# The product x2 W2 moved to the head of a neighbour search, with the loads behind the search reordered

## The chip, the cores and the metric

The kernel runs on one core of a Trainium2 chip. The metric is the device time of one execution in microseconds (us). Before the change the median of three runs is 1454.12 us (1453.49 to 1454.47).

## What is computed

Four graph layers in a row on x, 4096 nodes by 128 features, with a dense 4096 x 4096 matrix A. Each has the form x <- layernorm(x + layer(x)). The third and the fourth are the ones that matter here:

```
# layer 2: x2 goes in, x3 comes out
z   = leaky_relu(lap(A, x2) @ W1 + b1)                 # lap(A, x) = d * (A @ (d * x)), d = rowsum(A)^-1/2
S   = exp(-dist(z, z) / 2), kept for the 4 nearest rows of each row, else 0
out = lap(S + A, x2) @ W2 + b2                         # d from rowsum(S + A)
x3  = layernorm(x2 + out)
# layer 3
x4  = layernorm(x3 + relu(concat(x3, A @ x3) @ W.T + b))
```

## The kernel before

**Products.** The kernel makes six products with A, numbered 0 to 5 in the code (`p`); product five is `p = 4` (A with the scaled x2) and product six is `p = 5` (A with x3). Every f32 operand is split in a high and a low f16 half, so a tile of 128 rows of A costs three matmuls (L1144 to L1146) for each chunk of 512 output columns. There are 32 row tiles (`kt`) and 8 chunks. The first 7 row tiles of A stay in SBUF (`kept`); the other 25 lie in HBM (`at_scratch`) and are loaded either as units of 5 tiles (1280 KB, `load_late`, L417) into a ring of 5 slots, or as single tiles (256 KB, L428) into 8 tile slots.

**Search.** Between product four and five stands the search for the 4 nearest rows: 32 rows of tiles, `i` = 0 to 31. For each row TensorE makes 8 banks of closeness values (`first_banks`, `second_banks`, L1297 to L1299 and L1304), ScalarE (ACT) copies the banks from PSUM to SBUF (`copy_near`, L682), and VectorE (DVE) takes the 8 largest of each line and their places (`search`, L1028 and L1029). From row 8 on TensorE does beside it the first four chunks of product five (`wide_products`, row tile `i - 8`), whose operand becomes known four row tiles at a time: a group `g` of four rows goes through POOL (`distances`, `degree_sums`, `scales`, `low_y`), ACT (`weights`, `degrees`, `high_y`) and DVE (`inverse`), and the scaled x2 is written in two f16 halves, `yop`.

**x2 W2.** The sparse part of the product needs rows of (d * x2) W2 in HBM (`y_scratch`). In the kernel before it is made group by group during the search: POOL loads x2 (`load_x2`, L501), TensorE transposes it (`pe_turn`, L1093), ACT copies the transpose (L712), TensorE multiplies by W2 (`pe_project_x2`, L1120), ACT scales by d (`scale_yw`, L729) and POOL stores it (L548). The last group's part of this stands behind the search.

**Behind the search.** POOL loads x2 once more as residual (four loads, L558), and then issues 128 gathers of rows of `y_scratch` (L569), 16 for each chunk. DVE mixes them chunk by chunk: `mix_tile` (L837, L839), `close_mix` (layernorm and the split in halves, L798 and L799, which make product six's operand), and `residual` (L831), which reads the projected product five from PSUM. TensorE makes the rest of product five, chunks 4 to 7 (`chunk_columns`), and at places written out by hand (`PROJECT4_AT`) the projection of a finished chunk by W2 (`pe_project`, L1113). `pe_project` of chunk c waits until DVE's `residual` has read chunk c - 1 (`nat_read`); `RESIDUAL_AT` puts `residual` of chunk 3 behind the first mixed tile of chunk 1:

```python
RESIDUAL_AT = {(0, 2): [0], (0, 3): [1], (0, 4): [2], (1, 1): [3], **{(c, 3): [c + 3] for c in range(1, 5)}}
```

SP's queue carries the single tiles and all units in one order; the first three units stand between the tiles of the last rows (`LATE_AT`), the others wait until the first four chunks are done and the last group of y is stored.

Of the kernel before, what the change touches and what calls it, by code (L numbers as in the profile page):

```python
# [21 lines left out]
F32 = mybir.dt.float32  # L22
# [7 lines left out]
P = 128  # L30
# [13 lines left out]
LATE_ORDER = [4, 3, 2, 0, 1]  # L44
# [6 lines left out]
WIDE_AT = {i: i - 8 for i in range(8, 32)}  # L51
# [6 lines left out]
PROJECT4_AT = {(4, 9): 0, (4, 15): 1, (4, 21): 2, (4, 28): 3, (5, 12): 4, (6, 12): 5, (7, 12): 6}  # L58
# [3 lines left out]
WIDE_REST = [24, 25, 26, 27, 28, 29, 30, 31]  # L62
LATE_AT = {29: 0, 30: 1, 31: 2}
# [4 lines left out]
Y_SCALE = {-1: 256.0, 0: 16.0, 1: 128.0, 2: 512.0, 3: 512.0, 4: 128.0}  # L68
# [3 lines left out]
def gnn_kernel(nc, x, adj, d_list, w0, filt, bias0, alpha, w1, b1, wz, bz, w2, b2, w3, b3, out):  # L72
# [14 lines left out]
    y_dram = nc.dram_tensor("y_scratch", [N, D], F32).ap()  # L87
    part_dram = nc.dram_tensor("part_scratch", [NCH, P, CHUNK], F32).ap()

    with ExitStack() as ctx:  # L90
# [33 lines left out]
        x2_in = [chunk_buffer(s) for s in range(2)]  # L124
        yw = [chunk_buffer(2 + s) for s in range(2)]
        assert (REGION_TILES + 4) * tile_elems <= near_end - 4 * N

# [82 lines left out]
        util_nat = pt[3][:, :].rearrange("p (t f) -> p t f", t=TPC)  # L210
# [36 lines left out]
        dinv_ready, yhi_ready, yw_full, yw_ready = sem("dinv_ready"), sem("yhi_ready"), sem("yw_full"), sem("yw_ready")  # L247
        x2_loaded = [sem(f"x2_loaded{b}") for b in range(2)]
# [96 lines left out]

        block = ctx.enter_context(nc.Block())
# [3 lines left out]
        def _(sp):  # L350
# [61 lines left out]
            def load_late(k):  # L412
                p, c, u = LATE[k]
                slot = LATE_SLOTS[k]
                if slot in LATE_SLOTS[:k]:
                    sp.wait_ge(*late_released(max(b for b in range(k) if LATE_SLOTS[b] == slot)))
                sp.dma_start(ring[slot].rearrange("p k h n -> p (k h n)"), at_dram[c, u, :, :]  # L417
                             ).then_inc(late_loaded_unit[slot], 16)
# [27 lines left out]
        def _(pool):  # L446
# [53 lines left out]
            def load_x2(g):  # L500
                pool.dma_start(x2_in[g % 2], rows(x_dram[2], g)).then_inc(x2_loaded[g % 2], 16)  # L501

            pool.wait_ge(acc_full, 4 * NCH)
            load_x2(0)
            load_x2(1)
# [25 lines left out]
            def scales(g_tiles, g):  # L531
                pool.wait_ge(dinv_ready, g + 1)
                nc.gpsimd.tensor_tensor(S[:, g_tiles, :], S[:, g_tiles, :], dinv2[:, g_tiles].unsqueeze(2)
                                        .to_broadcast([P, TPC, TOP]), ALU.mult).then_inc(S_scaled, 1)

            def low_y(g_tiles, g):
                pool.wait_ge(yhi_ready, g + 1)
                pool.wait_ge(xT_full, nth(XT, 4, g))
                x2 = x2_in[g % 2]
                step(nc.gpsimd.tensor_tensor(x2, x2, dinv2y[:, g_tiles].unsqueeze(2).to_broadcast([P, TPC, D]), ALU.mult))  # L540
                nc.gpsimd.tensor_tensor(yop[1][:, 1, g_tiles, :], x2, yop[1][:, 0, g_tiles, :], ALU.subtract
                                        ).then_inc(yop_ready, 1)

            for g in range(NCH):
                for stage_of in (distances, degree_sums, scales, low_y):
                    stage_of(slice(g * TPC, (g + 1) * TPC), g)
                pool.wait_ge(yw_ready, g + 1)
                pool.dma_start(rows(y_dram, g), yw[g % 2]).then_inc(y_stored[g % 2], 16)  # L548
                if g + 2 < NCH:
                    pool.wait_ge(yop_ready, nth(YOP, "y", g))  # L550
                    pool.wait_ge(xT_full, nth(XT, 4, g))
                    load_x2(g + 2)


            pool.wait_ge(near_full, KT * NCH)
            x2_rows = x_dram[2].rearrange("(c t p) f -> p t c f", p=P, t=TPC)
            for t in range(TPC):
                pool.dma_start(res_rows(t // 2, 0, NCH)[:, :, t % 2, :], x2_rows[:, t, :, :]).then_inc(res_loaded, 16)  # L558
# [52 lines left out]
        def _(act):  # L611
# [96 lines left out]
            def turned_x2(g):  # L708
                act.wait_ge(xT_full, nth(XT, 4, g))
                if g > 0:  # L710
                    act.wait_ge(yw_full, g)
                nc.scalar.activation(xT[:, :], late_turn[:, :], ACT.Copy).then_inc(xT_ready, 1)  # L712

            def high_y(g):
                act.wait_ge(dinv_ready, g + 1)
                act.wait_ge(x2_loaded[g % 2], 16 * (g // 2 + 1))
                for t in range(TPC):
                    kt = g * TPC + t
                    last = nc.scalar.activation(yop[1][:, 0, kt, :], x2_in[g % 2][:, t, :], ACT.Copy,
                                                scale=dinv2y[:, kt:kt + 1])  # L720
                last.then_inc(yhi_ready, 1)

            def scale_yw(g):
# [770 lines left out]
```

## Time and profile before

| | before |
|---|---|
| median of 3 runs | 1454.12 us |
| time of the profiled execution | 1455.45 us |
| its span, first to last instruction | 1453.9 us |
| mean granted clock of TensorE | 0.990 |
| PE busy | 1392.0 us (96%) |
| DVE busy | 836.8 us (58%) |
| ACT busy | 450.9 us (31%) |
| POOL busy | 249.0 us (17%) |
| HBM | 277 GB/s over the span |

The span is one profiled execution; 1.5 us of its time lie around it. PE is TensorE's matmuls. A matmul's own time is longer than its distance to the next one, since they are pipelined, so the stages are read from starts and from idle time. Granted clock 1.00 is 2.4 GHz and 0.50 is 1.2 GHz.

### The profile page before, as it was taken

The page shows a single profiled execution, that of the slowest core. Times are in us where ns is not written, and L with a number is a line of the kernel's source. Part 1 is how long each engine was busy: PE and PEld are TensorE (multiplying, and loading weights), DVE is VectorE, ACT ScalarE, POOL GpSimd, SP SyncE. Part 2 cuts the span into 40 slices and gives each one's busy share as a digit, 9 for nine tenths or more (in the row PEclk, how much of TensorE's full clock was granted, in tenths as well). Part 3 has the DMA queues.
Part 4 walks back from the last instruction along what each step waited for, and adds up shares of the span by engine and source line. Part 5 has one row for each costly group of instructions (what it writes and reads, how often), then busy time and mean ns, then how long its engine had stood idle before and what let it go on. Part 6 is the DMA issues. An engine that isn't in the chain of part 4 may idle for free.

```text
span 1453.9 us, 20144 instructions
## 1 busy us (share of the span) xinstructions
PE 1392.0 (96%) x7300; PEld 738.1 (51%) x7300; DVE 836.8 (58%) x1311; ACT 450.9 (31%) x979; POOL 249.0 (17%) x358
## 2 busy tenths in 40 slices
PE   6999999999999999999999987999999889999997
PEld 4666676666544444444445432444444344444454
DVE  6877766666223523333222379999999356555044
ACT  4666665655200000000000045666666200000011
POOL 2111110110101100000000000111111277774000
PEclk9999999999999999999999999999999989999999
DMA  9999998897999979988878420004444799999961
GB/s 302 394 375 391 352 326 322 316 308 256 356 385 364 350 282 398 396 324 323 307 278 326 190 73 1 15 30 131 131 131 123 249 377 397 374 396 392 353 247 57
DMA packets 112818, 403.32 MB, mean 277 GB/s; under 512 B 10368, under 2 KB 28384, under 8 KB 91232
## 3 DMA queue, kind: packets, MB, share of 16 engines
q1 hardware_dynamic: 72672, 314.33, 58.2%
q0 software_dynamic: 20576, 77.07, 14.1%
q10 hardware_dynamic: 19488, 10.80, 2.4%
q8 instruction: 54, 0.88, 0.2%
q14 instruction: 28, 0.23, 0.0%
HBM read 337.67 MB, written 64.49 MB: 277 GB/s over the span
## 4 chain that ended last, share of the span: by engine, by line
PE 77%; DMA 10%; DVE 9%; ACT 1%; issue 1%; ACTq 0%; SPq 0%; DVEq 0%; POOL 0%; POOLq 0%
PE acc L1144 10%; PE acc L1146 9%; PE acc L1145 9%; PE pt L1208 5%; PE pt L1146 5%; PE pt L1145 5%; PE pt L1144 5%; DMA region<-in_adj 4%; PE pt L1297 3%; PE pt L1299 3%; PE pt L1298 3%; DVE hT L1028 3%; DMA region<-at_scratch 3%; PE acc L1189 2%; PE acc L1191 2%; PE acc L1193 2%
## 5 line engine op out<-in xcount | busy, mean ns | idle before, releaser
L1208 PE MATMUL pt<-ident,region 128*128 128x128 f32 x1024 | 243.8, 278 | 21.4 <-DMA region<-in_adj 12.9
L1144 PE MATMUL acc<-region,yop 128*128 128x512 f16 x581 | 221.3, 381 | 10.9 <-DMA region<-at_scratch 10.9
L1146 PE MATMUL acc<-region,yop 128*128 128x512 f16 x581 | 221.2, 381 | 0.0
L1145 PE MATMUL acc<-region,yop 128*128 128x512 f16 x581 | 221.2, 381 | 0.0
L974 DVE SCALAR_TENSOR_TENSOR region<-pt,region 128x512 f16<-128x512 f32 x200 | 135.5, 687 | 77.0 <-ACT region L636 76.7
L1208 PEld LDWEIGHTS pt<-ident,region 128*128 128x128 f32 x1024 | 146.2, 143 | 64.2 <-issue 14.7
L682 ACT ACTIVATE region<-pt 128x512 f32<-128x512 f32 x256 | 132.8, 603 | 109.5 <-PE pt L1304 95.8
L636 ACT ACTIVATE region<-pt 128x512 f16<-128x512 f32 x200 | 117.5, 595 | 108.3 <-PE pt L1208 89.4
L1028 DVE MAX8 hT<-region 128x8 f32<-128x4096 f32 x32 | 141.2, 4411 | 2.4 <-ACT region L682 2.4
L603 ACT ACTIVATE std<-mv,eps_ln 128x4 f32<-128x4 f32 x32 | 9.5, 297 | 343.0 <-DVE mv L808 343.0
L1297 PE MATMUL pt<-yop 128*128 128x512 f16 x256 | 97.3, 380 | 15.5 <-ACT region L682 15.5
L1144 PEld LDWEIGHTS acc<-region,yop 128*128 128x128 f16 x581 | 56.9, 98 | 80.6 <-issue 11.7
L1298 PE MATMUL pt<-yop 128*128 128x512 f16 x256 | 97.0, 379 | 0.0
L1299 PE MATMUL pt<-yop 128*128 128x512 f16 x256 | 97.0, 379 | 0.0
L469 POOL DMA_DIRECT2D at_scratch<-region x80 | 42.7, 534 | 314.2 <-DVE region L974 304.5
L1144 PE MATMUL pt<-region,yop 128*128 128x512 f16 x250 | 94.8, 379 | 0.0
L1145 PE MATMUL pt<-region,yop 128*128 128x512 f16 x250 | 94.8, 379 | 0.0
L1146 PE MATMUL pt<-region,yop 128*128 128x512 f16 x250 | 94.8, 379 | 0.0
L1146 PEld LDWEIGHTS acc<-region,yop 128*128 128x128 f16 x581 | 57.0, 98 | 69.2 <-issue 1.1
L1145 PEld LDWEIGHTS acc<-region,yop 128*128 128x128 f16 x581 | 56.9, 98 | 62.5 <-issue 0.3
L986 DVE TENSOR_REDUCE rs_part<-region 128x1 f32<-128x512 f32 x128 | 86.5, 676 | 0.0
L1193 PE MATMUL acc<-region,yop 128*128 128x512 f16 x200 | 75.8, 379 | 0.0
(236 smaller groups left out, 2239.6 us busy)
## 6 DMA issues: line engine op xcount, KB each, us to landing
region<-at_scratch SPq DMA_DIRECT2D x166, 1280.0 KB, 8.1
region<-in_adj SPq DMA_DIRECT2D x64, 1024.0 KB, 9.3
at_scratch<-region POOLq DMA_DIRECT2D x40, 768.0 KB, 7.1
at_scratch<-region POOLq DMA_DIRECT2D x40, 512.0 KB, 7.6
region<-at_scratch SPq DMA_DIRECT2D x76, 256.0 KB, 2.8
x_scratch<-xout ACTq DMA_DIRECT2D x16, 256.0 KB, 13.7
gath_all<-x_scratch POOLq DMA_DIRECT2D x12, 256.0 KB, 6.6
xin<-at_scratch SPq DMA_DIRECT2D x12, 256.0 KB, 2.7
```

The source lines that it names most:

```text
L636: nc.scalar.activation(dst, pt[kt % 4][:, :], ACT.Copy, scale=A_SCALE).then_inc(high_done, 1)
L682: nc.scalar.activation(near[i % 2][:, j * CHUNK:(j + 1) * CHUNK], near_bank(i, j)[:, :], ACT.Copy).then_inc(near_copied, 1)
L974: nc.vector.scalar_tensor_tensor(lo, pt[kt % 4][:, :], A_SCALE, hi, ALU.mult, ALU.subtract).then_inc(low_done, 1)
L1028: step(nc.vector.max(top8[:, i, :], near[i % 2]))
L1144: nc.tensor.matmul(into, y[:, 0, kt, :], high, start=(kt == first_tile), stop=False)
L1145: nc.tensor.matmul(into, y[:, 0, kt, :], low, start=False, stop=False)
L1146: return nc.tensor.matmul(into, y[:, 1, kt, :], high, start=False, stop=(kt == last_tile))
L1193: last = nc.tensor.matmul(acc[par][:, :], yl, hi, start=False, stop=(kt == KT - 1))
L1208: ins = nc.tensor.transpose(pt[kt % 4][:, t * P:(t + 1) * P], nat[u % 4][:, t, (kt % TPC) * P:(kt % TPC + 1) * P], ident[:, :])
L1297: nc.tensor.matmul(into, zh, zT[:, 0, cols], start=True, stop=False)
L1298: nc.tensor.matmul(into, zh, zT[:, 1, cols], start=False, stop=False)
L1299: nc.tensor.matmul(into, zl, zT[:, 0, cols], start=False, stop=False)
```

## The change

x2 W2 is made without the scaling by d in search rows 1 to 4, stored in a new HBM tensor (`xw_scratch`) and loaded again group by group. The scaled rows (d times it) now serve both as the rows that are gathered and as product five's operand, so product five comes out already multiplied by W2 and `pe_project` only transposes it. The wide columns lag the search by 7 rows and not 8. The four residual loads go from POOL's queue to SP's; units 0 to 3 go from SP's queue to ACT's; two units of chunk 4 are used between the wide rows; `inverse` and `high_y` come one row earlier. The core of the diff:

```diff
-LATE_ORDER = [4, 3, 2, 0, 1]
+LATE_ORDER = [4, 3, 2, 1, 0]
...
-WIDE_AT = {i: i - 8 for i in range(8, 32)}
+WIDE_LAG = 7
+WIDE_AT = {i: i - WIDE_LAG for i in range(WIDE_LAG, 32)}
...
-PROJECT4_AT = {(4, 9): 0, (4, 15): 1, (4, 21): 2, (4, 28): 3, (5, 12): 4, (6, 12): 5, (7, 12): 6}
+PROJECT4_AT = {(4, 17): 0, (4, 21): 1, (4, 25): 2, (4, 29): 3, (5, 12): 4, (6, 12): 5, (7, 12): 6}
...
-LATE_AT = {29: 0, 30: 1, 31: 2}
+ACT_LATE = 4
+RES_AT = 26
@@ SP
+            sp.wait_ge(z_ready, NCH)
+            for g in range(NCH + 2):
+                if g > 0 and g < NCH:
+                    sp.wait_ge(xT_full, nth(XT, 4, g - 1))
+                if g < NCH:
+                    sp.dma_start(t_nat[:, :, :], rows(x_dram[2], g)).then_inc(x2_loaded, 16)
+                if g >= 2:
+                    sp.wait_ge(xw_ready, g - 1)
+                    sp.dma_start(rows(xw_dram, g - 2), xw_out[g % 2]).then_inc(xw_stored[g % 2], 16)
...
             for kt in range(KEPT, KT):
+                if kt == RES_AT:
+                    sp.wait_ge(near_full, KT * NCH)
+                    for t in range(TPC):
+                        sp.dma_start(res_rows(t // 2, 0, NCH)[:, :, t % 2, :], x2_rows[:, t, :, :]).then_inc(res_loaded, 16)
...
-                if kt in LATE_AT:
-                    sp.wait_ge(near_used, KT - 1 if LATE_AT[kt] == 0 else KT)
-                    load_late(LATE_AT[kt])
...
             sp.wait_ge(acc_full, nth(ALL, 4, WIDE - 1))
-            sp.wait_ge(yop_ready, nth(YOP, "y", NCH - 1))
-            sp.wait_ge(xT_full, nth(XT, 4, NCH - 1))
-            for b in range(2):
-                sp.wait_ge(y_stored[b], 16 * NCH // 2)
-            for k in range(len(LATE_AT), len(LATE)):
-                load_late(k)
+            for k in range(ACT_LATE, len(LATE)):
+                load_late(sp, k)
@@ POOL
             for g in range(NCH):
-                for stage_of in (distances, degree_sums, scales, low_y):
+                for stage_of in (distances, degree_sums, scaled_y, low_y, scales):
                     stage_of(slice(g * TPC, (g + 1) * TPC), g)
-                pool.wait_ge(yw_ready, g + 1)
                 pool.dma_start(rows(y_dram, g), yw[g % 2]).then_inc(y_stored[g % 2], 16)
...
-            pool.wait_ge(near_full, KT * NCH)
-            for t in range(TPC):
-                pool.dma_start(res_rows(t // 2, 0, NCH)[:, :, t % 2, :], x2_rows[:, t, :, :]).then_inc(res_loaded, 16)
@@ ACT
+            def copy_xw(g):
+                act.wait_ge(xw_full, g + 1)
+                if g >= 2:
+                    act.wait_ge(xw_stored[g % 2], 16 * (g // 2))
+                nc.scalar.activation(xw_out[g % 2].rearrange("p t f -> p (t f)"), acc[1][:, :], ACT.Copy, scale=Y_SCALE[3]
+                                     ).then_inc(xw_ready, 1)
...
+            def projection_step(k):
+                if 0 < k <= NCH:
+                    copy_xw(k - 1)
+                if k < NCH:
+                    turned_x2(k)
...
+            projection_step(0)
+            for i in range(1, KT + TPC + 1):
+                if i == KT:
+                    act.wait_ge(near_used, KT - 1)
+                    load_late(act, 0)
+                if i == KT + 1:
+                    act.wait_ge(near_used, KT)
+                    load_late(act, 1)
+                    load_late(act, 2)
...
+                projection_step(2 * i - 1)
                 if i < KT:
                     copy_near(i, COPY_ORDER[NEAR_BANKS:])
+                projection_step(2 * i)
...
+            act.wait_ge(yop_ready, nth(YOP, "y", NCH - 1))
+            for b in range(2):
+                act.wait_ge(y_stored[b], 16 * NCH // 2)
+            load_late(act, ACT_LATE - 1)
@@ TensorE
-                if p == 1:
+                if p in (1, 4):
                     last = nc.tensor.transpose(into[:, t, :], h, ident[:, :])
...
             for i in range(1, KT):
                 first_banks(i)
+                projection_step(2 * i - 1)
+                if i == WIDE_LAG:
+                    pe.wait_ge(xw_ready, NCH)
                 if i in WIDE_AT and i < KT - 1:
                     wide_products(WIDE_AT[i], range(WIDE // 2))
                 second_banks(i)
+                projection_step(2 * i)
...
+            kept_narrow(NARROW_KEPT[0])
+            wide_products(25)
+            kept_narrow(NARROW_KEPT[1])
+            wide_products(26)
+            wide_products(27)
+            chunk_columns(4, WIDE, range(KEPT, KEPT + 2 * UNIT))
+            for kt in range(28, KT):
                 wide_products(kt)
```

On TensorE `projection_step(k)` multiplies group k - 1 by W2 (`pe_project_x2`) and transposes group k (`pe_turn`).

## Rows read from the trace of the kernel before

**Rows 1.** Windows by stage: busy us (count) per engine, clock, DMA share, GB/s.

```profile
851.50:914.00 62.50, 47.45 (x248) 18.47 (x247) 62.18 (x24) 33.76 (x68) 3.94 (x10) 1.00 0.02 7
914.00:1120.00 206.00, 205.60 (x1080) 89.70 (x1078) 204.87 (x82) 129.48 (x264) 31.10 (x70) 1.00 0.32 98
1120.00:1146.00 26.00, 25.04 (x127) 12.45 (x128) 17.69 (x8) 12.57 (x30) 7.11 (x14) 1.00 0.43 136
1146.00:1175.00 29.00, 17.92 (x54) 5.44 (x53) 2.53 (x3) 0.53 (x1) 14.46 (x16) 0.73 1.01 355
1175.00:1284.00 109.00, 109.00 (x534) 53.85 (x533) 69.91 (x161) 5.74 (x13) 84.01 (x83) 0.99 0.99 385
1284.00:1384.00 100.00, 100.00 (x469) 45.90 (x467) 31.31 (x72) 2.08 (x5) 37.07 (x39) 1.00 0.97 377
```

**Rows 2.** Windows again: two stretches at a lowered clock.

```profile
1156.00:1169.00 13.00, 9.10 (x21) 2.50 (x21) 0.00 (x0) 0.00 (x0) 6.70 (x7) 0.50 1.03 380
1173.00:1177.00 4.00, 4.00 (x11) 1.42 (x12) 3.93 (x4) 0.60 (x1) 3.63 (x2) 0.58 0.96 369
```

**Rows 3.** Timeline of DVE, search: start, us, line, operation, tiles, [idle before].

```profile
851.55 4.43 DVE L1028 MAX8 hT<-region 128x8 f32<-128x4096 f32 x1 [2.42 <-ACT region L682]
...
1132.99 4.42 DVE L1029 FIND_INDEX8 wT<-hT,region 128x8 uint32<-128x4096 f32 x1
1141.81 0.18 DVE L1034 RECIPROCAL inv_deg<-dinv 128x4 f32<-128x4 f32 x1 [4.40 <-ACT dinv L706]
```

**Rows 4.** Timeline of PE, row one of the search.

```profile
854.69 0.39 PE L1297 MATMUL pt<-yop 128*128 128x512 f16 x1 [0.68 <-ACT region L682]
...
858.95 0.39 PE L1297 MATMUL pt<-yop 128*128 128x512 f16 x1 [1.17 <-ACT region L682]
```

**Rows 5.** Timeline of PE, behind the search: one of six waits.

```profile
1156.14 0.61 PE L1144 MATMUL acc<-region,yop 128*128 128x512 f16 x1 [2.91 <-DMA region<-at_scratch]
```

**Rows 6.** Timeline of POOL, behind the search.

```profile
1143.58 1.04 POOL L540 TENSOR_TENSOR region<-region,scale 128x512 f32<-128x512 f32 x1 [1.09 <-ACT yop L719]
...
1145.80 0.82 POOL L548 DMA_DIRECT2D y_scratch<-region  x1
1146.62 2.67 POOL L558 DMA_DIRECT2D yop<-x_scratch  x3
1160.46 0.90 POOL L558 DMA_DIRECT2D yop<-x_scratch  x1 [11.18 <-issue]
1161.67 1.06 POOL L569 DMA_INDIRECT gath_all<-y_scratch,wz_sb  x1 [0.31 <-issue]
...
1183.58 0.94 POOL L569 DMA_INDIRECT gath_all<-y_scratch,wz_sb  x1 [0.30 <-issue]
```

**Rows 7.** Source view of L548, stores of y.

```profile
DMA to landing us min/median/max: 2.8/2.8/5.7
```

**Rows 8.** Timeline of DVE, first mixed chunk.

```profile
1189.87 0.69 DVE L837 TENSOR_TENSOR gath_all<-gath_all,bias 128x512 f32<-128x512 f32 x1 [2.43 <-DMA gath_all<-y_scratch,wz_sb]
...
1197.00 0.74 DVE L799 SCALAR_TENSOR_TENSOR yop<-xout,yop 128x512 f16<-128x512 f32 x1
...
1199.34 1.12 DVE L831 SCALAR_TENSOR_TENSOR yop<-pt,inv_deg,yop 128x128 f32<-128x128 f32 x4
```

**Rows 9.** Timeline of PE, projection of chunk four in product five.

```profile
1200.86 1.05 PE L1113 MATMUL pt<-w_sb,hT 128*128 128x128 f32 x8
```

**Rows 10.** Chain of waits, a projection: start, us, what.

```profile
1201.02 0.89 PE pt L1113 x8
```

**Rows 11.** Chain of waits, four transposes in place of one.

```profile
402.02 0.44 PE pnat L1107 x4
```

**Rows 12.** DMA issues from 840 to 1200: queue, count, KB each, us to landing.

```profile
region<-at_scratch SPq DMA_DIRECT2D x10, 1280.0 KB, 9.9
...
region<-x_scratch POOLq DMA_DIRECT2D x8, 256.0 KB, 3.5
...
yop<-x_scratch POOLq DMA_DIRECT2D x4, 512.0 KB, 10.3
```

More of the change, by code:

```diff
@@ L122, in chunk_buffer @@
             return region[:, at:at + tile_elems].bitcast(F32).rearrange("p (t f) -> p t f", t=TPC)
-        x2_in = [chunk_buffer(s) for s in range(2)]
+        xw_in = [chunk_buffer(s) for s in range(2)]
         yw = [chunk_buffer(2 + s) for s in range(2)]
         assert (REGION_TILES + 4) * tile_elems <= near_end - 4 * N
+        xw_out = [tiles[REGION_TILES - 2 + s].rearrange("p h n -> p (h n)").bitcast(F32)
+                  .rearrange("p (t f) -> p t f", t=TPC) for s in range(2)]
         yop = [sb(f"yop{b}", [P, 2, KT, D], F16) for b in range(2)]
@@ L344, in load_x0, with load_late @@
             eng.dma_start(x0[:, part, :], x.rearrange("(t p) f -> p t f", p=P)[:, part, :]).then_inc(x0_loaded[q], 16)
+        def load_late(eng, k):
+            p, c, u = LATE[k]
+            slot = LATE_SLOTS[k]
+            if slot in LATE_SLOTS[:k]:
+                eng.wait_ge(*late_released(max(b for b in range(k) if LATE_SLOTS[b] == slot)))
+            eng.dma_start(ring[slot].rearrange("p k h n -> p (k h n)"), at_dram[c, u, :, :]
+                          ).then_inc(late_loaded_unit[slot], 16)
         block = ctx.enter_context(nc.Block())
@@ L557, in _ @@
[L557 to L558 removed]
+                    load_xw(g + 2)
             pool.wait_ge(near_used, KT)
@@ L721, in high_y @@
                 last.then_inc(yhi_ready, 1)
-            def scale_yw(g):
-                act.wait_ge(yw_full, g + 1)
-                if g >= 2:
-                    act.wait_ge(y_stored[g % 2], 16 * (g // 2))
-                for t in range(TPC):
-                    kt = g * TPC + t
-                    last = nc.scalar.activation(yw[g % 2][:, t, :], util_nat[:, t, :], ACT.Copy,
-                                                scale=dinv2[:, kt:kt + 1])
-                last.then_inc(yw_ready, 1)
@@ L733, in _ @@
-            for i in range(KT + TPC + 1):
-                if 0 < i < KT:
+            def projection_step(k):
[12 more added lines that the diff above has]
+                    load_late(act, 2)
+                g, step_of = divmod(i - TPC - 1, TPC)
+                if i < KT:
@@ L737, in _ @@
                     copy_near(i, COPY_ORDER[:NEAR_BANKS])
[L738 to L742 removed]
                 if g >= 0 and step_of == 0:
[L744 to L745 removed]
                     weights(g)
                 if g >= 0 and step_of == 1:
+                    high_y(g)
+                projection_step(2 * i - 1)
+                if i < KT:
+                    copy_near(i, COPY_ORDER[NEAR_BANKS:])
+                projection_step(2 * i)
+                if g >= 0 and step_of == 0:
                     degrees(g)
[L749 to L752 removed]
+            act.wait_ge(yop_ready, nth(YOP, "y", NCH - 1))
+            for b in range(2):
+                act.wait_ge(y_stored[b], 16 * NCH // 2)
+            load_late(act, ACT_LATE - 1)
             act.wait_ge(xT_ready, nth(XTS, 4, NCH - 1))
@@ L1041, in _ @@
                 g, step_of = divmod(i - TPC + 1, TPC)
-                if g >= 0 and step_of == 2:
+                if g >= 0 and step_of == 1:
                     inverse(g)
@@ L1118, in pe_project_x2 @@
             pe.wait_ge(xT_ready, nth(XTS, 4, g))
+            if g > 0:
+                pe.wait_ge(xw_ready, g)
             for t in range(TPC):
-                last = nc.tensor.matmul(util_nat[:, t, :], xT[:, t * P:(t + 1) * P], w2_sb[:, :], start=True, stop=True)
-            last.then_inc(yw_full, 1)
+                last = nc.tensor.matmul(xw_nat[:, t, :], xT[:, t * P:(t + 1) * P], w2_sb[:, :], start=True, stop=True)
+            last.then_inc(xw_full, 1)
         def pe_squares(pe, c, par):
@@ L1416, in _ @@
                     pe.wait_ge(hT_ready, nth(ALL, 4, c - 2))
-                for kt in range(KEPT if c in NARROW_KEPT else 0, KT):
+                for kt in range(KEPT + 2 * UNIT if c == WIDE else KEPT if c in NARROW_KEPT else 0, KT):
                     last = chunk_columns(4, c, [kt])
```

113 lines of the change are left out of this document (41 added, 72 removed).

## The prediction

> **What bounds the kernel now.** I read the windows by stage first. In the search, 851.5 to 1137, DVE works without a break; behind row 8 PE is as full as DVE, 205.6 and 204.87 us of 206 [rows 1]. From 1175 to 1384 PE has no idle time at all. The one hole lies between: from 1146 to 1175 PE is busy for 17.92 us of 29, at a mean clock of 0.73, while DMA is full (share 1.01, 355 GB/s) [rows 1]. The PE timeline shows what the hole is: TensorE waits for tiles of A, 2.91 us in the longest wait but one [rows 5], and then runs at the lower level, 0.50 over 13 us and 0.58 over 4 us [rows 2]. So two things are late behind the search: tiles for TensorE, and, on POOL's timeline, the gathers. The fourth residual load is held up for 11.18 us before it can be issued, and the first gather starts at 1161.67, although the last y went out at 1145.80 [rows 6]. The reader should hold these two apart, since the change moves both, and they meet again when TensorE has to wait for DVE's `residual`, at the projection of chunk 4.
>
> **First search rows.** Eight times 0.44 us of transposes and 0.89 us of products [rows 10, 11], 10.7 us, come into rows 1 to 4, and with them two loads, two stores and four ACT copies a row. PE idles there for 62.5 - 47.45 = 15.05 us over seven rows [rows 1], 0.68 + 1.17 us of it in row one [rows 4]. The two steps of a row take 2 x 1.33 = 2.66 us, so they overrun these gaps by 0.8 us. A row cost DVE (1137.41 - 851.55) / 32 = 8.93 us [rows 3], and PE's part of it is 47.45 / 7 = 6.8 us, 9.4 with the two steps if nothing of it overlaps and 8.9 if it fills the gaps. ACT has the room (33.76 us of 62.5 [rows 1]). Bounds of the delay to the search: 0, and 4 x 0.5 = 2 us. I take 0, since matmul times overlap and PE's busy sum is therefore too high. The single x2 buffer makes load, transpose and next load serial: with the median 3.5 us of such a load [rows 12] two of them take 2 x (3.5 + 0.44) = 7.9 us a row, under 8.93. This is the tightest new wait; see the rivals.
>
> **Later search rows.** From row 7 PE loses 1.33 us in four rows. DVE then sets the row alone, and it had 206 - 204.87 = 1.1 us of idle time [rows 1], so at most 1.1 us can come of it; I take 0 and leave the search's end at 1132.99 + 4.42 = 1137.41 [rows 3]. `inverse` and `high_y` a row earlier feed the shorter lag; they are hidden behind the search.
>
> **TensorE's own path behind the search.** One wide row (12 matmuls at 0.213 us, from 100 us / 469 [rows 1]) is done earlier: 2.6. The last two products and the last transpose of x2 go: 2 x 0.89 + 0.44 = 2.2. If no tile is late, the idle time of the hole goes, 29 - 17.92 = 11.1, and the half clock, 9.10 / 2 = 4.6 and 4.0 x 0.42 = 1.7 [rows 1, 2]. Four projections before chunk 4's become transposes, 4 x 0.45 = 1.8 [rows 10, 11]. Together 24.0: TensorE could stand at the projection of chunk 4 at 1200.86 - 24.0 = 1176.9 [rows 9]. This is the ceiling, not the forecast.
>
> **The gather chain.** That projection waits for DVE's `residual` of chunk 3, which ends at 1199.34 + 1.12 = 1200.46, 0.4 us before the projection starts at 1200.86 [rows 8, 9]. PE shows no wait there, but has nothing in hand either. So I follow what comes before that residual:
>
> The multiplication of 1.04 us that stood behind the high half [rows 6] now runs beside it, and a smaller scaling comes in: y goes out 0.8 us earlier (0 to 1.04), at 1145.0. Its landing took 2.8 to 5.7 us [rows 7]; DMA is full there, so 4.9: 1149.9. With the residual loads gone from POOL the gathers start then, 11.8 us earlier (1145.8 + 5.7 gives 10.2, 1144.8 + 2.8 gives 14.1). The first sixteen took 1183.58 + 0.94 - 1161.67 = 22.85 us [rows 6]; at the spacing of the last of them, 0.94 + 0.30, sixteen take 19.6. The surplus of 3.2 fell while the fourth residual load was still in POOL's queue. I take 3.1 (0 to 3.2). From the sixteenth gather to the end of chunk 3's residual nothing changes: landing, mixing, the first layernorm, 1184.52 to 1200.46, with the split of chunk 0 at 1197.00 on the way [rows 8]. I allow 1.5 us either way for the landing. So the residual ends 14.9 us earlier, at 1185.6, and PE can project chunk 4 at 1185.7: 15.2 us earlier, later than the 1176.9 of its own path. The gathers bind, and 8.8 us of what TensorE gains is waited away, in pieces: each projection of chunks 1 to 4 waits for DVE.
>
> **Clock.** Such pieces could lower the clock. In the hole 2.91 us of waiting [rows 5] was followed by 0.50 [rows 2]. What is slow before the last handoff is waited away anyway; only slow matmuls behind it count: 0, or at most 4.0 x 0.42 = 1.7 us and a little more as between 1173 and 1177 [rows 2]. I take 0.7. The Trainium skill, "TensorE: Matmul & The Clock Gate", section "HAM oscillation — how this bites in real kernels", says that a matmul stream broken by DMA waits falls back to the slow clock each time; the hole agrees (0.50), and by that rule the sum below would be 1438.8 and not 1437.8.
>
> **Loads.** Between the last search row and chunk 4's second half lie 4 residual loads of 512 KB, 24 tiles of 256 KB and 4 units of 1280 KB: 2.1 + 6.3 + 5.2 = 13.6 MB, 38 us at 355 GB/s [rows 1, 12]. They can begin when the last four closeness banks are made, which starts when row 29 is searched, 2 x 8.93 = 17.9 us before the search's end, and takes 858.95 - 1.17 - 854.69 = 3.1 us [rows 4]: at about 1123. So they last to 1161; before, DMA moved 136 GB/s from 1120 to 1146 [rows 1], and the earlier units use that. On PE's own path, 1176.9 less 21 row tiles of chunks 4 and 5 (3 x 0.213 us each [rows 1]) and four transposes [rows 11], the wide rows are done at 1161.7. There is no slack in that, but the 8.8 us of waiting behind it takes a delay. I cost it at 0; uncovered, every us beyond 8.8 counts in full. The tiles of row tiles 26 and on stand behind the residual loads in SP's queue, and `weights` of the last group behind two issues on ACT's, which the distances on POOL hide.
>
> **The sum.** 15.2 + 4 x 0.45 for the transposes from chunk 4 on - 0.7 = 16.3 us. Against the profiled execution, 1455.45 (span 1453.9 and 1.5 around it), 1439.1; its time is 1.3 above the median, so 1454.12 - 16.3 = 1437.8. Product six stays as it is: PE and DMA are full there (0.97 to 0.99 [rows 1]), and its operand comes earlier with the gathers.
>
> **The rivals.**
> TensorE's own path binds: y lands in 2.8 us and the gathers run quickly, or the handoffs are looser than they look. For it: the bound of 14.1 + 3.2 + 1.5 = 18.8. Against it: 0.4 us at chunk 4. Time: up to 24.0 + 1.8 = 25.8 less, 1428.3; halfway to the forecast, 1433.
> The loads give it back: two queues share what was full already. For it: 38 us of bytes in 38 us; against it, the 8.8 us. If the 13.6 MB need 52 us (262 GB/s), TensorE is 14 late, 5.2 beyond the cover, and about 2 more by the clock: 1445; if the hole stays as it is, only 4.8 + 3.6 = 8.4 is left: 1446. The Trainium skill, "DMA: Bandwidth & Descriptors", section "Issuing engines are not separate DMA queues", says that loads from another engine's queue run on the same 16 DMA engines and save only issue time. By that rule the units on ACT's queue bring nothing but their earlier start; the share of 1.01 in the hole agrees.
> Slower: the serial x2 loads hold the search. From 4.0 us a load on, 2 x (L + 0.44) passes a row's 8.93, and each us more costs 2 us in each of four rows. At 6.1 us the whole 16.3 is gone; at the 10.3 us that the 512 KB loads took [rows 12] it costs 4 x (21.5 - 8.93) = 50 us: 1488. For it: only 0.5 us of room at the median. Against it: DMA's share is 0.02 there [rows 1], and an SP issue is cheaper than POOL's.
> No gain: something else holds DVE's first chunk at its old time, so that chunk 4 is projected at 1200.86 as before; only 1.8 remain, 1452, within 0.2% of the old time.
>
> **How the numbers follow.** Gather chain 0.6 (own range 1433.5 to 1445.3: 18.8 + 1.8 less at the one end, 10.2 + 0 - 1.5 + 1.8 - 1.7 = 8.8 less at the other); TensorE's path 0.12; loads 0.17; slower 0.06; no gain 0.05. The range 1430 to 1446 leaves out the last two and the far end of the others. A measurement of this kernel tells 0.2%, 2.9 us, from no change. Faster 0.89, same 0.05, slower 0.06.
>
> **What would show it.** Right: search's end within 2 us of 1137.4; first gather at 1148 to 1152; sixteenth 19.6 us behind it; transposes of chunk 4 at 1184 to 1188, right behind chunk 3's residual; short PE waits on DVE before them. Wrong: MAX8 rows with idle time before row 5; PE waits for tiles longer than 9 us in all; first gather after 1155; the chunk 4 transposes well behind the residual, which would make the loads or TensorE the bound.

## The result and the profile after

The changed kernel takes 1442.02 us (median of five runs, 1441.11 to 1444.95) against 1454.12 (five runs, 1451.0 to 1459.46): a ratio of 0.9926, 95% interval 0.9909 to 0.9943. That is 12.1 us by the medians, where 16.3 were forecast; the time lies inside the stated range of 1430 to 1446. Measured again later, it took 1443.95 (0.9928, 0.9910 to 0.9945).

The windows by stage of the changed kernel (columns as in [rows 1]):

```profile
849.20:911.70 62.50, 58.61 (x340) 29.61 (x338) 61.02 (x23) 41.17 (x82) 6.94 (x14) 1.00 0.38 114
911.70:1119.00 207.30, 203.31 (x1018) 79.45 (x1016) 206.30 (x83) 121.26 (x239) 31.73 (x71) 1.00 0.32 101
1119.00:1145.00 26.00, 25.76 (x122) 11.52 (x123) 17.55 (x8) 8.29 (x17) 4.65 (x11) 1.00 0.88 299
1145.00:1174.00 29.00, 22.57 (x99) 9.32 (x97) 8.97 (x10) 1.79 (x3) 18.27 (x16) 0.94 0.88 334
1174.00:1284.00 110.00, 105.44 (x487) 49.07 (x488) 69.00 (x166) 4.47 (x10) 83.98 (x86) 0.97 0.99 380
```

The first rows of the search now hold 11.2 us more of PE. The hole behind it shrank: 22.57 us busy of 29 at a clock of 0.94, where [rows 1] have 17.92 at 0.73. DMA moves 299 GB/s around the search's end where it moved 136. New is the idle time of PE in the last stage, 4.56 us of 110, where there was none.

PE's timeline behind the search; the bracket is the idle time and what ended it:

```profile
1150.30 0.39 PE L1168 MATMUL acc<-xin,yop 128*128 128x512 f16 x1 [1.31 <-DMA xin<-at_scratch]
1157.74 0.38 PE L1168 MATMUL acc<-region,yop 128*128 128x512 f16 x1 [2.73 <-DMA region<-at_scratch]
1159.33 0.61 PE L1168 MATMUL acc<-xin,yop 128*128 128x512 f16 x1 [0.78 <-DMA xin<-at_scratch]
1169.72 0.63 PE L1129 MATMUL pt<-ident,hT 128*128 128x128 f32 x4 [0.55 <-DVE yop L856]
1177.11 1.09 PE L1129 MATMUL pt<-ident,hT 128*128 128x128 f32 x4 [4.18 <-DVE yop L856]
1190.19 0.63 PE L1129 MATMUL pt<-ident,hT 128*128 128x128 f32 x4 [1.45 <-DVE yop L856]
```

TensorE still waits for tiles, 4.82 us in three pieces, but what it waits for last is DVE: 6.18 us before the transposes (L1129) of chunks 1, 2 and 4, each right behind the residual of the chunk before; those of chunk 3, at 1182.96, came without a wait, 0.7 us behind the residual of chunk 2. DVE's `residual` of chunk 3 ends at 1188.93 + 1.12 = 1190.05, 0.14 us before the transposes of chunk 4:

```profile
1188.93 1.12 DVE L856 SCALAR_TENSOR_TENSOR yop<-pt,inv_deg,yop 128x128 f32<-128x128 f32 x4
```

POOL's timeline, to be held against [rows 6]:

```profile
1143.78 0.82 POOL L569 DMA_DIRECT2D y_scratch<-region  x1
1150.97 1.06 POOL L582 DMA_INDIRECT gath_all<-y_scratch,wz_sb  x1 [6.37 <-DMA y_scratch<-region]
1152.33 0.98 POOL L582 DMA_INDIRECT gath_all<-y_scratch,wz_sb  x1 [0.30 <-issue]
...
1162.35 2.88 POOL L582 DMA_INDIRECT gath_all<-y_scratch,wz_sb  x1 [0.30 <-issue]
1165.54 2.02 POOL L582 DMA_INDIRECT gath_all<-y_scratch,wz_sb  x1 [0.31 <-issue]
...
1172.86 0.94 POOL L582 DMA_INDIRECT gath_all<-y_scratch,wz_sb  x1 [0.30 <-issue]
```

The residual loads are gone from here, and what POOL waits for is the last store of y. Its source view gives the landing times of the eight stores, for [rows 7]:

```profile
DMA to landing us min/median/max: 2.8/3.6/6.3
```

And DVE's search, for [rows 3]:

```profile
849.24 4.43 DVE L1053 MAX8 hT<-region 128x8 f32<-128x4096 f32 x1 [2.42 <-ACT region L695]
858.64 4.43 DVE L1053 MAX8 hT<-region 128x8 f32<-128x4096 f32 x1 [0.45 <-ACT region L695]
...
895.05 0.18 DVE L1059 RECIPROCAL inv_deg<-dinv 128x4 f32<-128x4 f32 x1 [0.65 <-ACT dinv L719]
...
1131.85 4.42 DVE L1054 FIND_INDEX8 wT<-hT,region 128x8 uint32<-128x4096 f32 x1
```

The search starts at 849.24 here and at 851.55 before. That is no effect of the change: over the fourteen profiled executions of this study it starts between 846.90 and 855.07. So I count from the search's start, or from its end T (1137.41 before, 1136.27 after). Each term of the forecast beside its measurement:

| term | forecast | measured, from the rows |
|---|---|---|
| search longer | 0 | 1.17 (287.03 for 285.86) |
| last y issued earlier, from T | 0.8 | 0.88 (T + 7.51 for T + 8.39) |
| y issued to first gather | 4.9 | 7.19 |
| first gather earlier, from T | 11.8 | 9.56 (T + 14.70 for T + 24.26) |
| first sixteen gathers | 19.6 | 22.83 |
| chunk 3's residual ends earlier, from T | 14.9 | 9.26 (T + 53.78 for T + 63.04) |
| transposes of chunk 4 earlier, from T | 15.2 | 9.53 (T + 53.92 for T + 63.45) |
| from there to the end, shorter | 1.1 | 2.76 (250.26 for 253.02) |
| sum | 16.3 | 9.53 + 2.76 - 1.17 = 11.12 |

The two profiled executions lie 1455.45 - 1442.02 = 13.43 us apart; the 2.31 us beyond the sum are the earlier start of the search.

### The profile page after: what moved, and what is told of

Same layout as the page of the kernel before. It is cut to its first block, busy times and chain, and to the rows that moved or that the text cites. A ratio compares the mean times of both kernels' runs of the same rounds, so it can differ in the third digit from the quotient of the medians.

```text
span 1440.5 us, 20058 instructions
## 1 busy us (share of the span) xinstructions
PE 1389.3 (96%) x7268; PEld 731.8 (51%) x7268; DVE 835.8 (58%) x1311; ACT 445.5 (31%) x955; POOL 243.7 (17%) x354
## 3 DMA queue, kind: packets, MB, share of 16 engines
q10 hardware_dynamic: 20064, 16.04, 3.3%
## 4 chain that ended last, share of the span: by engine, by line
PE 66%; DVE 21%; DMA 8%; ACT 2%; POOL 1%; issue 1%; ACTq 0%; DVEq 0%; SPq 0%; POOLq 0%
PE acc L1168 9%; PE acc L1170 9%; PE acc L1169 9%; DVE hT L1053 8%; PE pt L1232 6%; DVE wT L1054 5%; PE pt L1168 4%; PE pt L1170 4%; PE pt L1169 4%; DMA region<-in_adj 4%; DVE wz_sb L1054 3%; PE acc L1213 3%; PE acc L1217 3%; PE acc L1215 3%; PE pxT L1204 1%; PE pxT L1205 1%
```

## The experiments

Theory G is the prediction's: the gathers, DVE's mixing and its residuals set when TensorE can go on at chunk 4. Rivals are that the loads set it, and that one part of the change alone does it all. Times are medians; ratios are to the kernel before, run beside.

**One part undone, one part alone.** First the changed kernel with the residual loads back in POOL's queue:

```diff
-                if kt == RES_AT:
-                    sp.wait_ge(near_full, KT * NCH)
-                    for t in range(TPC):
-                        sp.dma_start(res_rows(t // 2, 0, NCH)[:, :, t % 2, :], x2_rows[:, t, :, :]).then_inc(res_loaded, 16)
...
+            pool.wait_ge(near_full, KT * NCH)
...
+            for t in range(TPC):
+                pool.dma_start(res_rows(t // 2, 0, NCH)[:, :, t % 2, :], x2_rows[:, t, :, :]).then_inc(res_loaded, 16)
```

> The changed kernel with one part undone: the four residual loads stand in POOL's queue again, between the last store of y and the gathers, and no longer in SP's queue. Theory G (the gathers, through DVE's residual reads, set when TensorE may go on): the first gather starts some 10 us later behind the search's end than in the changed kernel, chunk 3's residual too, and the time goes from 1442 to 1450 to 1454. Rival L (tiles and units of A set it): SP's tiles of rows 26 to 31 come earlier, TensorE's waits for tiles (4.8 us in the changed kernel) shrink, and the time is 1437 to 1442.

It took 1453.45 (0.9998, 0.9983 to 1.0014), as theory G had it: the gain is gone. POOL's timeline shows how:

```profile
1144.84 0.82 POOL L564 DMA_DIRECT2D y_scratch<-region  x1
1145.65 2.67 POOL L572 DMA_DIRECT2D yop<-x_scratch  x3
1160.81 0.90 POOL L572 DMA_DIRECT2D yop<-x_scratch  x1 [12.49 <-issue]
1162.01 1.06 POOL L583 DMA_INDIRECT gath_all<-y_scratch,wz_sb  x1 [0.31 <-issue]
```

Three loads go out in 2.67 us, the fourth is held up for 12.49 us with nothing to wait for that the profile shows, and the first gather comes at T + 24.68, where it was before. Everything else of the change is still in.

What ends the hold can be read from the landings. In the kernel before the third load is issued at 1148.4 and takes 11.7 us to land:

```profile
L558 POOL DMA_DIRECT2D yop<-x_scratch x1: 904/904/904, 1148.4 to 1148.4; - x1
DMA to landing us min/median/max: 11.7/11.7/11.7
```

So it lands at 1160.1, and the fourth is issued at 1160.46 [rows 6]. Here the third is issued at 1147.4, lands 13.0 us later, at 1160.4, and the fourth follows at 1160.81. In both kernels the fourth goes out 0.4 us after the third has landed. Two cases do not show why; four loads in POOL's queue at another time were not tried.

Then the kernel before with that one move and nothing else:

```diff
+            x2_rows = x_dram[2].rearrange("(c t p) f -> p t c f", p=P, t=TPC)
...
+                if kt == 26:
+                    sp.wait_ge(near_full, KT * NCH)
+                    for t in range(TPC):
+                        sp.dma_start(res_rows(t // 2, 0, NCH)[:, :, t % 2, :], x2_rows[:, t, :, :]).then_inc(res_loaded, 16)
...
-            pool.wait_ge(near_full, KT * NCH)
-            x2_rows = x_dram[2].rearrange("(c t p) f -> p t c f", p=P, t=TPC)
-            for t in range(TPC):
-                pool.dma_start(res_rows(t // 2, 0, NCH)[:, :, t % 2, :], x2_rows[:, t, :, :]).then_inc(res_loaded, 16)
```

> The kernel before with this one part of the change alone: the residual loads go from POOL's queue to SP's, ahead of row tile 26. Theory G: gathers start about 10 us earlier, but TensorE's own hole behind the search stays, and at chunk 4 it had only 0.4 us in hand over DVE; so the gathers alone give 0 to 3 us: 1451 to 1454. A third reading, that the gathers alone set the time, gives 1444. Rival L: the tiles stand behind four more loads, the hole grows, 1454 to 1458.

It took 1444.11 (0.9932, 0.9909 to 0.9954), the time of the third reading; theory G as I had applied it gave 0 to 3 us. So one of the parts holds nearly all of the gain, and without it the others bring nothing. SP's, POOL's and PE's timelines, and the window of PE's hole:

```profile
1122.27 5.95 SPq L426 DMA_DIRECT2D yop<-x_scratch  x4
...
1147.80 1.06 POOL L568 DMA_INDIRECT gath_all<-y_scratch,wz_sb  x1 [5.83 <-DMA y_scratch<-region]
...
1189.75 1.05 PE L1112 MATMUL pt<-w_sb,hT 128*128 128x128 f32 x8
...
1141.40:1170.40 29.00, 20.84 (x85) 8.28 (x83) 9.19 (x11) 1.19 (x2) 18.59 (x17) 0.88 0.95 352
```

My figure for G failed because it kept PE's hole as it was. The hole shrank too: PE is busy for 20.84 us of 29 at a clock of 0.88, where it was 17.92 at 0.73 [rows 1], and its waits for tiles behind the search come to 8.15 us in five pieces, where they were 11.07 in six. The loads go out at 1122.27, when the DMA engines had been a third busy. The first gather is at T + 15.04. The residual of chunk 3 ends at T + 54.7, and TensorE is at its projection of chunk 4 at T + 57.0 (T + 63.45 in the kernel before), 2.3 us behind that residual: here its own path binds, as the ceiling of the prediction had it for the other parts to lift.

**Half the gathers.** The changed kernel with two of the four gathers of each tile left out (DVE still mixes four):

```diff
-                    for r in range(TOP):
+                    for r in range(TOP // 2):
...
-                dve.wait_ge(gath_loaded[t], 16 * TOP * (c + 1))
+                dve.wait_ge(gath_loaded[t], 16 * TOP // 2 * (c + 1))
```

> The changed kernel with two of the four gathers of each tile left out (DVE mixes four as before, two of them from whatever lies in the buffer): a probe of the gather chain's price. Theory G: chunk 0 is gathered some 11 us earlier, TensorE's waits for DVE (0.55, 4.18 and 1.45 us) and the half clock behind them (6.8 us at half, 3.4 lost) go, and what is left is TensorE's own path: 1432 to 1437. Rival L: 1440 to 1443, since the loads of A are what they were.

It took 1437.4 (0.9879, 0.9857 to 0.9902). DVE's and PE's timelines:

```profile
1183.57 1.12 DVE L856 SCALAR_TENSOR_TENSOR yop<-pt,inv_deg,yop 128x128 f32<-128x128 f32 x4
...
1184.84 0.63 PE L1129 MATMUL pt<-ident,hT 128*128 128x128 f32 x4 [0.75 <-DVE yop L856]
```

The residual of chunk 3 ends at T + 45.29, 8.5 us earlier, the transposes of chunk 4 follow at once (T + 45.4), and of PE's 6.18 us of waiting for DVE 0.75 are left. The chain binds, as G says. The time is a little above G's range; the tile waits (4.58 us) stay. It shows 4.6 of the 8.5 us: in the profiled execution the search starts 2.8 us later than in that of the changed kernel, and the search and the stretch behind the handoff are 0.3 and 0.7 us longer.

**The handoffs later.** Transposes of chunks 1 to 5 put later among chunk 4's, 5's and 6's columns, so that TensorE reaches them when the residual is there:

```diff
-PROJECT4_AT = {(4, 17): 0, (4, 21): 1, (4, 25): 2, (4, 29): 3, (5, 12): 4, (6, 12): 5, (7, 12): 6}
+PROJECT4_AT = {(4, 17): 0, (4, 23): 1, (5, 10): 2, (5, 18): 3, (5, 29): 4, (6, 14): 5, (7, 12): 6}
```

> The changed kernel with TensorE's transposes of the finished chunks placed later by hand: chunk 1 at row tile 23 of chunk 4, chunks 2, 3 and 4 at 10, 18 and 29 of chunk 5, chunk 5 at 14 of chunk 6. Nothing else moves, the gathers least of all. Theory G: TensorE no longer stands waiting for DVE's residual reads; the 6.2 us and the half clock behind them go, 1433 to 1438, less if product six then has to wait for its operand. Rival L: 1440 to 1443, with as much more waiting for units of A.

It took 1445.29 (0.9944, 0.9924 to 0.9965): no gain, where theory G said 1433 to 1438. The waits for DVE are gone, and PE's timeline has others:

```profile
1210.26 0.66 PE L1129 MATMUL pt<-ident,hT 128*128 128x128 f32 x4 [4.11 <-ACT hT L609]
...
1250.18 0.39 PE L1168 MATMUL pt<-kept,yop 128*128 128x512 f16 x1 [2.17 <-ACT hT L609]
```

I tried it once more with only chunks 3, 4 and 5 moved:

```diff
+PROJECT4_AT = {(4, 17): 0, (4, 21): 1, (4, 25): 2, (5, 10): 3, (5, 24): 4, (6, 14): 5, (7, 12): 6}
```

> The changed kernel with the transposes of chunks 3 and 4 alone put later into chunk 5's columns (after its row tiles 10 and 24) and those of chunk 5 two tiles later in chunk 6, so that TensorE has columns to do while DVE's residuals of chunks 2 and 3 are late. Theory G (the 4.2 and 1.5 us of TensorE's waits for those two residuals are worth what they last): both waits go, 1437 to 1440. Theory L (the loads of units and the rest of the gathers' chain, which the earlier run with all handoffs later met, take the wait over): the waits come back at units and at ScalarE's hT, 1441 to 1446.

It took 1444.5 (0.9923, 0.9904 to 0.9942), the same as the changed kernel, and in the range of theory L. The expectation names the 4.18 us wrongly: they stand before the transposes of chunk 2, which this edit leaves where they were. Here TensorE does not wait there, since the residual of chunk 1 ends at T + 38.0, where it was T + 40.7. In place of the three waits for DVE, 6.18 us, PE has one of 4.37, and ACT's timeline shows why:

```profile
1250.66 0.61 PE L1168 MATMUL pt<-kept,yop 128*128 128x512 f16 x1 [4.37 <-ACT hT L609]
```

```profile
1247.81 0.30 ACT L616 ACTIVATE std<-mv,eps_ln 128x4 f32<-128x4 f32 x1 [18.11 <-DVE mv L833]
1249.55 0.37 ACTq L621 DMA_DIRECT2D x_scratch<-xout  x1
1250.01 0.60 ACT L609 ACTIVATE hT<-pt 128x512 f32<-128x512 f32 x1 [1.91 <-DVE xout L840]
```

ACT writes `hT` of chunk 7 only behind its part of chunk 3's layernorm, and that waits 18.11 us for DVE, which stands still for 7.8 of them until gathers have landed. The same chain stops TensorE at another handoff. Moving ACT's `hT` ahead of that layernorm (`SUMS_AHEAD` 5) together with these handoffs was not tried.

**Where the residual loads cost.** Two of the four back in POOL's queue, two left in SP's:

```diff
-                    for t in range(TPC):
+                    for t in range(TPC // 2):
...
+            pool.wait_ge(near_full, KT * NCH)
...
+            for t in range(TPC // 2, TPC):
+                pool.dma_start(res_rows(t // 2, 0, NCH)[:, :, t % 2, :], x2_rows[:, t, :, :]).then_inc(res_second, 16)
```

> The changed kernel with two of the four residual loads (1 MB of the 2 MB) put back into POOL's queue, behind the last store of y; the other two stay in SP's queue, ahead of row tile 26. Theory Q (it is the issue of the fourth load that is held up in POOL's queue, 11.2 and 12.5 us in the kernels that have all four there, and with it the gathers behind it): two loads are issued in 0.9 us each without a hold, the first gather goes out when y has landed, 15 to 17 us behind the search's end, and the time is 1441 to 1445. Theory D (what counts is when those 2 MB go through the DMA engines, which are full from the search's end on): half of the 10 us that the residual loads in POOL's queue cost comes back, first gather or not, so 1446 to 1449.

POOL's timeline behind the last y:

```profile
1145.84 0.82 POOL L569 DMA_DIRECT2D y_scratch<-region  x1
1146.65 1.79 POOL L576 DMA_DIRECT2D yop<-x_scratch  x2
1152.72 1.06 POOL L587 DMA_INDIRECT gath_all<-y_scratch,wz_sb  x1 [4.28 <-DMA y_scratch<-region]
```

There is no hold: two loads in 1.79 us, and the first gather at T + 14.40, when y has landed. The time is 1446.84 (0.9953, 0.9933 to 0.9972; eleven runs from 1441.81 to 1451.35), above Q's figure and at D's. In the profiled execution, 1444.19 us, the transposes of chunk 4 start at T + 53.5, as early as in the changed kernel; where the median lost the rest is not shown.

And all four in SP's queue, but at row tile 29, so that they go out behind the search's end:

```diff
-RES_AT = 26
+RES_AT = 29
```

> The changed kernel with the residual loads still in SP's queue, but ahead of row tile 29 in place of 26, so that they go out at about the time at which POOL issued them in the kernel before (5 to 10 us behind the search's end) and not 14 us ahead of it. Theory Q (what the residual loads cost in POOL's queue is that the fourth one holds up the gathers): the first gather stays at 14 to 16 us behind the search's end and the time at 1441 to 1445. Theory D (what counts is that their 2 MB go through the DMA engines before the search ends, when the engines are a third busy): 1447 to 1452, with the first gather early all the same and TensorE waiting for tiles and units instead.

It took 1446.35 (0.9945, 0.9927 to 0.9962), between the two. SP's, POOL's and PE's timelines:

```profile
1141.87 11.76 SPq L445 DMA_DIRECT2D yop<-x_scratch  x4
1153.67 6.03 SPq L452 DMA_DIRECT2D region<-at_scratch  x5
```

```profile
1152.97 1.06 POOL L582 DMA_INDIRECT gath_all<-y_scratch,wz_sb  x1 [6.18 <-DMA y_scratch<-region]
```

```profile
1164.27 0.58 PE L1168 MATMUL acc<-region,yop 128*128 128x512 f16 x1 [11.15 <-DMA region<-at_scratch]
```

Now SP is held up, 11.76 us for four issues that took 3.91 at row tile 26, and TensorE waits 11.15 us for a tile. Yet it reaches the transposes of chunk 4 at T + 53.4, as early as in the changed kernel, because the gathers started at T + 14.51. So most of the gain, from 0.9998 to 0.995, comes from freeing the gathers of the hold in POOL's queue. The rest, from 0.995 to 0.993, may come from sending the 2 MB ahead of the search's end; the intervals overlap, and that stays open.

**The last store of y.** Three attempts to bring it in sooner: the third unit of ACT's queue issued behind it (e6), the store issued ahead of `low_y` and `scales` (e8), and the store issued from ACT's queue (e11):

```diff
 # e6
-                    load_late(act, 2)
...
             for b in range(2):
                 act.wait_ge(y_stored[b], 16 * NCH // 2)
+            load_late(act, 2)
 # e8
-                for stage_of in (distances, degree_sums, scaled_y, low_y, scales):
+                for stage_of in (distances, degree_sums, scaled_y):
                     stage_of(slice(g * TPC, (g + 1) * TPC), g)
                 pool.dma_start(rows(y_dram, g), yw[g % 2]).then_inc(y_stored[g % 2], 16)
+                for stage_of in (low_y, scales):
+                    stage_of(slice(g * TPC, (g + 1) * TPC), g)
 # e11
...
-                    load_late(act, 2)
...
+            act.wait_ge(y_made, 1)
+            act.dma_start(rows(y_dram, NCH - 1), yw[(NCH - 1) % 2]).then_inc(y_last, 16)
+            load_late(act, 2)
```

> The changed kernel with the third unit of ScalarE's queue (1280 KB) issued only when all of y has landed, in place of 0.4 us behind the second. Theory N (the 7.1 us that the last store of y takes to land, where the quiet stores of before took 2.8, is time in line behind the units and row tiles that were issued ahead of it): y lands 2 to 4 us earlier, the first gather goes out at 11 to 13 us behind the search's end instead of 14.7, the residual of chunk 3 and the transposes of chunk 4 follow, and the time is 1438 to 1441, unless PE waits for the late unit. Rival F (the store's landing is a fixed time of POOL's queue, or is set by the tiles of SP's queue alone): the first gather stays at 14 to 15 us, and the time is 1441 to 1444.

> The changed kernel with each store of y issued right behind the multiplication that makes it, ahead of the split into the low half and the scaling of S: the last store is issued 1.4 us earlier. Theory G (the chain from y's landing to the first sixteen gathers sets the time): first gather and transposes of chunk 4 1 to 1.4 us earlier, 1440.4 to 1441.2, a ratio of 0.999 to the changed kernel. Rival F (the store lands when the DMA engines let it): nothing earlier, 1441.5 to 1443.

> The changed kernel with the last store of y issued from ScalarE's queue, behind its second unit and ahead of its third, in place of POOL's queue. Theory S (the 7 to 8 us to landing belong to a store in POOL's queue beside full queues of SP and ScalarE): it lands in 3 to 5 us, the first gather goes out 11 to 13 us behind the search's end in place of 14.7, and the time is 1438 to 1441. Theory F (any store waits that long while the DMA engines are full): first gather at 14 to 17 us, 1441 to 1445.

| kernel | median | ratio (interval) | y issued | first gather | transposes of chunk 4 |
|---|---|---|---|---|---|
| changed | 1442.02 | 0.9926 (0.9909 to 0.9943) | T + 7.51 | T + 14.70 | T + 53.9 |
| e6 | 1445.72 | 0.9947 (0.9929 to 0.9965) | T + 7.50 | T + 16.04 | T + 54.8 |
| e8 | 1443.59 | 0.9936 (0.9918 to 0.9954) | T + 6.39 | T + 14.48 | T + 53.2 |
| e11 | 1446.85 | 0.9939 (0.9918 to 0.9960) | T + 5.98 | T + 14.44 | T + 53.7 |

None brings anything: issued up to 1.5 us earlier, from either queue, y is there at about the same time. By the first gather rival F comes nearest in all three, though e6 lies 1.0 us behind its 15 and the three medians 0.6 to 1.9 us above its times. Neither the unit beside the store nor POOL's queue makes the 7 us. While the store is under way, the share of DMA is 0.92 (e6), 1.02 (e8) and 1.06 (e11), and 1.01 in the changed kernel.

**The lag.** The wide columns eight rows behind, as before the change:

```diff
-WIDE_LAG = 7
+WIDE_LAG = 8
...
+            wide_products(24)
```

> The changed kernel with the wide columns eight rows behind again: the products of one more row tile, 2.6 us, lie behind the search. Theory G (the chain of gathers, mixing and residuals sets when TensorE can go on behind chunk 4, and TensorE waits 6.2 us for it): the 2.6 us fill some of the wait, the transposes of chunk 4 stay at 53 to 55 us behind the search's end, and the time stays at 1441 to 1444. Rival P (TensorE's own path or the loads of row tiles bind): 1444 to 1446.

It took 1445.09 (0.9949, 0.9926 to 0.9972), by the median in P's range, by the interval in both: the time does not decide. The trace speaks for G: the transposes of chunk 4 start at T + 54.2 as ever, and of the 6.18 us of waiting for DVE 0.45 are left. The 2.6 us of columns and longer tile waits (8.84 us) took its place. The repeat of the changed kernel has them at T + 54.2 as well:

> The changed kernel itself, run beside the next three, so that they are compared on one chip at one time: 1440 to 1444, a ratio to the kernel before of 0.990 to 0.994, and the first gather at 14 to 15.5 us behind the search's end.

It took 1443.95 (0.9928), with the first gather at T + 15.07 and DVE waits of 6.25 us.

## Why the prediction came out as it did

**The mechanism was right.** After the change the gather chain binds at chunk 4, right behind chunk 3's residual, and TensorE waits in pieces for DVE (6.18 us; 8.8 forecast), before chunks 1, 2 and 4. Half the gathers (e3) moved the handoff by 8.5 us. Two of the signs that were to show it missed, both through the next two terms: the sixteenth gather came 22.8 us behind the first and not 19.6, and the transposes of chunk 4 came at 1190.19 and not by 1188.

**The term of the first sixteen gathers failed.** The prediction laid their surplus, of which it took off 3.1 us, to the fourth residual load in POOL's queue. It is there without that load: 22.83 us after, 22.85 before, and both hold two long gathers, 2.88 and 2.02 us after and in the kernel before

```profile
1174.32 2.88 POOL L569 DMA_INDIRECT gath_all<-y_scratch,wz_sb  x1 [0.30 <-issue]
1177.50 2.03 POOL L569 DMA_INDIRECT gath_all<-y_scratch,wz_sb  x1 [0.30 <-issue]
```

The kernel before could have told it: its fourth load is issued at 1160.46 and lands 10.5 us later, at 1171.0, ahead of both. From the first gather to the end of chunk 3's residual it took 37.3 to 39.7 us in every kernel with all gathers. This term cost 3.1 of the 5.7 us by which the handoff was forecast too early.

**The landing of y was mis-sized.** Forecast 4.9 us between bounds of 2.8 and 5.7 [rows 7]; measured 7.19 from issue to first gather. Of the 2.3 us too little, 1.4 are the landing, 6.3 us. The 5.7 belongs to the last store of the kernel before. The windows of the two stores, before and after, show how full the DMA engines were (last two columns):

```profile
1145.80:1151.50 5.70, 4.94 (x23) 1.88 (x20) 0.00 (x0) 0.00 (x0) 3.48 (x5) 1.00 0.93 295
1143.78:1150.08 6.30, 5.20 (x25) 2.16 (x22) 0.00 (x0) 0.00 (x0) 0.82 (x2) 1.00 1.01 393
```

The other 0.9 lie between the landing and the first gather, which the prediction put at nothing; in the twelve kernels whose first gather waits for y they are 0.87 to 0.90.

**Search: 0 forecast, 1.17 measured.** DVE's idle time before row 1 (0.45) and before the first `inverse` (0.65) is 1.10 of it; both stood within the bounds of the prediction's two steps together. The two parts that all twelve changed kernels share, x2 W2 at the head and `inverse` a row earlier, bring them, and not the lag: the search takes 286.87 to 287.61 us in the twelve (287.52 in e7, with the lag of before) and 285.86 in the kernel before and in e2. Serial x2 loads did not hold it: they land in 2.8 us, and the last store of x2 W2 is issued in row 4. The rival that ended slower had no footing.

**TensorE's own path** was given all tiles in time in the ceiling; it waited 4.82 us for them. In e3, where DVE holds it least, it stands at chunk 4 at T + 45.4; without its 0.75 us of waiting for DVE and 4.58 for tiles that would be T + 40.1, close to the ceiling, 1176.9 or T + 39.5. The slack behind it covered that, as the prediction had it for the loads: e7 put 2.6 us more on this path, e10 a tile wait of 11.15, and the transposes of chunk 4 stayed within 0.5 us. The rival in which the loads give it back fell for this kernel, but there is little cover left: with TensorE earlier (e4, e12) it waits for units, 0.35 to 0.55 us at a time.

**The clock** was costed at 0.7 us behind the last handoff; it cost nothing there. Two windows of the changed kernel hold all of the half clock between the search's end and the last handoff:

```profile
1158.91:1162.32 3.41, 2.99 (x8) 1.02 (x9) 1.82 (x3) 0.00 (x0) 2.52 (x3) 0.50 0.95 330
1175.98:1182.81 6.83, 5.70 (x16) 2.63 (x17) 4.29 (x12) 0.60 (x1) 5.04 (x6) 0.50 1.01 394
```

Both follow waits (2.73 us before 1157.74, 4.18 before 1177.11) and lie ahead of the last handoff, 1190.19, so the gathers cover them; from 1190 to 1300 the clock is 1.00.

**Behind the last handoff** the 1.8 us of the four transposes came, and 0.96 us more. Those are luck: in the profiled execution of the kernel before DVE waits once for a store of `out_x`, and TensorE behind it for 1.14 us where its waits of this kind beside it, before and after, are 0.17 to 0.18 (the last one, 0.69 in both, apart); e2, whose code there is that of the kernel before, takes 252.02 us from its projection of chunk 4 to the end, 1.0 less.

```profile
1415.51 1.12 DVE L815 TENSOR_SCALAR xout<-t_nat,mv,rstd 128x128 f32<-128x128 f32 x4 [1.01 <-DMA out_x<-xout]
...
1418.34 0.49 PE L1109 MATMUL pt<-wT,xT 128*128 128x128 f32 x2 [1.14 <-ACT hT L596]
```

So 9.53 + 1.8 - 1.17 = 10.2 us of the profiled difference are the change's, where 16.3 were forecast; the late store and the start of the search brought the rest of the 13.43.

**What was not seen** is how lopsided the change is. The prediction's sum has the residual loads' move in it, in the 11.8 us of the first gather, but it laid the shrinking of PE's hole to the other parts, and never priced the move alone; e1 and e2 show that it carries nearly the whole gain by itself, with TensorE at chunk 4 6.4 us earlier (e2), and the x2 W2 work, the lag and the units' order together about 1 us, less than can be told. The Trainium skill, "DMA: Bandwidth & Descriptors", section "Issuing engines are not separate DMA queues", says that issuing from another engine saves only the time of initiating the DMA, which is usually small beside the DMA itself. For the units on ACT's queue the runs agree: with everything but the residual move, e1 gains nothing. For the residual loads the usual case does not hold: the fourth was held for 11.18 us before and 12.49 in e1, longer than the 10.3 us that such a load took to land [rows 12], and moving it off POOL's queue was most of the gain.

## What to carry to other kernels

Look at how long a DMA takes to be issued, not only to land: a load that is held up at issue stops all that its engine has behind it, so several large plain loads do not belong ahead of a chain of gathers in one queue. Before a change with many parts is costed as a whole, cost each part alone against the wait that ends last; here the move of four loads carried nearly all of it. And where a chain hands over at several places, making one handoff later only brings the next one up.

## What the runs showed of the hardware

- Issue of a DMA can stall on its queue with no semaphore to wait for: of four 512 KB loads of 512-byte rows in POOL's queue the fourth was held for 11.18 and 12.49 us, until 0.4 us after the third had landed; of two neither was held (e5). In SP's queue four took 3.91 us (5.95 in e2) ahead of the search's end and 11.76 behind it, where the share of DMA is 1.05 (e10).
- A 256 KB store lands in 2.8 us during the search, where the share of DMA is 0.32. Issued behind the search at a share of 0.92 to 1.06, from POOL's queue or ACT's, it took 5.7 to 7.6 us in the fourteen kernels; issued at T + 5.98 to T + 8.38, it let the first gather go at T + 14.4 to T + 16.0 in every kernel that did not hold the gathers.
- In every kernel two gathers in a row take 2.4 to 3.0 and 2.0 us to issue where most others take 0.94, some 9 to 13 us behind the first one. What makes them long was not found.
